# Attention values on one core: the last 17 keys as four 32-row tiles, straight from the transposed blocks

## The reference

```python
def reference(x, ctx_1024, mask, g_xattn, g_ffn, Wq, Wk, Wv, Wo, Wg, W1, W2, W3):
    q = (_layernorm(x) @ Wq).reshape(b, -1, 16, 64)
    k, v = (ctx @ Wk).reshape(b, -1, 16, 64), (ctx @ Wv).reshape(b, -1, 16, 64)
    scores = einsum('bthd,bThd->bhtT', q, k) / sqrt(64)
    scores = where(mask, scores, finfo(float32).min)
    x = x + tanh(g_xattn) * (einsum('bhtT,bThd->bthd', softmax(scores), v).reshape(b, t, 1024) @ Wo)
    n = _layernorm(x)
    top_v, top_i = top_k(n @ Wg.T, 2)
    ...
    y = (silu(n @ W1[e].T) * (n @ W2[e].T)) @ W3[e].T        # for each expert e
    x = x + tanh(g_ffn) * sum_e y * w_e
```

## Time and profile before

| | us |
|---|---|
| median of 3 runs | 617.12 |
| lowest, highest | 616.49, 617.38 |
| the profiled execution | 619.6 |
| its span, first to last instruction | 617.5 |
| TensorE busy | 594.6 (96%) |
| VectorE busy | 407.2 (66%) |
| ScalarE busy | 271.2 (44%) |
| GpSimd busy | 308.6 (50%) |
| mean granted TensorE clock | 0.99 |

### The profile page before, as it was taken

How to read it: one execution, slowest core, us unless ns; L and a number is a source line. 1 busy time by engine, 2 the same in 40 slices (tenths; PEclk the granted TensorE clock), 3 DMA queues, 4 the chain that set the end, 5 groups by cost and what they waited for, 6 DMA issues and landing times.

```text
span 617.5 us, 10982 instructions
## 1 busy us (share of the span) xinstructions
PE 594.6 (96%) x2914; PEld 348.6 (56%) x2915; DVE 407.2 (66%) x1271; ACT 271.2 (44%) x711; POOL 308.6 (50%) x272
## 2 busy tenths in 40 slices
PE   8999899999999999999999999999999999999993
PEld 5444464656556565555655565656656665666562
DVE  3777988898988989988899976257363322332221
ACT  3755665666565665665656554212421122112210
POOL 3753545565565698564796653612364322222221
PEclk9999999999999999999999989999999999999998
DMA  8936676676767879688787774899676443233312
GB/s 308 340 80 144 137 165 144 144 183 150 165 141 182 172 190 208 130 181 181 152 207 157 167 166 111 251 320 321 159 140 151 64 63 54 42 51 52 50 20 31
DMA packets 114243, 93.74 MB, mean 152 GB/s; under 512 B 38528, under 2 KB 108032, under 8 KB 114176
## 3 DMA queue, kind: packets, MB, share of 16 engines
q1 hardware_dynamic: 92096, 70.37, 47.2%
q10 hardware_dynamic: 15360, 13.64, 10.1%
q0 software_dynamic: 6720, 8.95, 8.8%
HBM read 27.72 MB, written 12.36 MB: 65 GB/s over the span
## 4 chain that ended last, share of the span: by engine, by line
PE 70%; DVE 15%; issue 5%; DMA 3%; ACT 3%; SPq 2%; ACTq 1%; POOL 0%; DVEq 0%; POOLq 0%
PE ps_s L1702 19%; PE ps_o L1518 12%; PE ps_o L1730 9%; PE ps_s L1469 9%; DVE blocksT L1185 5%; PE ps_a L1528 5%; DVE probs L1173 5%; PE ps_t L1406 4%; PE ps_t L1723 2%; ACT probs L748 2%; PE ps_o L1483 2%; PE ps_a L1406 2%; PE ps_t L1469 2%; PE ps_a L1437 1%; DMA out_dram<-yg,ids 1%
## 5 line engine op out<-in xcount | busy, mean ns | idle before, releaser
L615 POOL TENSOR_TENSOR probs<-probs,inv_sum 128x802 f32<-128x802 f32 x128 | 194.9, 1524 | 138.1 <-DVE inv_sum L1162 136.9
L748 ACT ACTIVATE probs<-probs,neg_max 128x401 f32<-128x401 f32 x256 | 159.3, 624 | 111.7 <-DVE neg_max L1173 111.6
L1702 PE MATMUL ps_s<-w_sb,xgT 128*128 x288 | 135.3, 593 | 0.0
L1173 DVE CUSTOM_DVE_ANT_0 probs<-ps_s,biases 128x401 f32<-128x401 f32 x215 | 116.0, 570 | 20.3 <-PE ps_s L1469 19.7
L1185 DVE STREAM_TRANSPOSE blocksT<-probs 128x832 f32<-128x832 f32 x124 | 129.0, 1040 | 0.3 <-POOL probs L615 0.3
L665 POOL DMA_INDIRECT out_dram<-yg,ids x36 | 56.1, 1558 | 141.2 <-DVE yg L1344 101.7
L1518 PE MATMUL ps_o<-probsT,v_sb 128*64 128x512 f32 x496 | 114.3, 603 | 0.0
L1469 PE MATMUL ps_s<-kT,qT 64*128 64x201 f32 (+1 forms) x860 | 109.4, 350 | 3.4 <-DVE neg_max L1173 2.7
L1469 PEld LDWEIGHTS ps_s<-kT,qT 64*128 64x128 f32 x860 | 85.0, 189 | 44.2 <-issue 28.8
L884 ACT COPY gatedT<-ps_t 128x512 f32<-128x512 f32 x36 | 21.1, 585 | 151.6 <-PE ps_t L1723 151.6
L1334 DVE TENSOR_TENSOR gated<-ps_s,silu 128x512 f32<-128x512 f32 x36 | 24.8, 690 | 86.8 <-PE ps_s L1702 82.3
(11 more groups left out here) (182 smaller groups left out, 526.1 us busy)
## 6 DMA issues: line engine op xcount, KB each, us to landing
probsT<-blocksT SPq DMA_DIRECT2D x276, 96.0 KB
probsT<-blocksT SPq DMA_DIRECT2D x92, 128.0 KB
probsT<-blocksT ACTq DMA_DIRECT2D x96, 96.0 KB
xg_blocks<-x_regrouped SPq DMA_DIRECT2D x156, 32.0 KB, 2.2
probsT<-blocksT ACTq DMA_DIRECT2D x32, 128.0 KB
w_sb<-W1T_dram SPq DMA_DIRECT2D x8, 512.0 KB, 5.0
w_sb<-W2T_dram SPq DMA_DIRECT2D x8, 512.0 KB, 5.9
w_sb<-W3T_dram SPq DMA_DIRECT2D x8, 512.0 KB, 8.2
```

What stands on the lines that cost most here:

```text
L615: pool.tensor_tensor(duo, duo, inv_sum[:, u:u + 2].unsqueeze(2).to_broadcast([P, 2, LASTK]), ALU.mult)\
L748: act.activation(probs[:, b, 0:LASTK], probs[:, b, 0:LASTK], ACT.Exp, bias=neg_max[:, b:b + 1], scale=-1.0, accum_out=sum_exp[:, b:b + 1]) ...
L1173: dve.tensor_tensor_reduce(probs[:, b, 0:LASTK], scores_bank(u)[:, 0:LASTK], biases[:, tile, :], HD ** -0.5, 3e38, ALU.add, ALU.min, neg_m ...
L1702: mm = pe.matmul(bank[:, :], xgT[:, buf, k, :], w_sb[:, bass.ds(expert, 1), (n * KT + k) * FH:(n * KT + k + 1) * FH].squeeze(1), start=(k ...
```

## The change

The three full strips are multiplied as before. The tail (the 13th block, 17 keys and 15 of zeros) isn't carried into `probsT` any more: `tail(c, b, ...)` takes block 12 of `blocksT` where it lies, on partitions 32b to 32b + 31, as a 32-row tile against 128 query columns, four times (b = 0 to 3) for each of the two heads. For that the values of the last 17 keys must stand on all four groups of 32 partitions. So a padded context `ctx_tail` with the 17 keys four times over is made by GpSimd at the start, and `values` multiplies it at full width.

Row tiles of different rows must not write one bank at the same time. In chunks 4 to 28 (`PAIRED`) the query columns are split over two banks, `ps_o` and `ps_t[1]`, strips are cut into halves of 256 columns, and tails 0 and 2, then 1 and 3 run side by side in the two banks. Tails into one bank wait for each other (`tail_added`). In chunks 0 to 3, 29 and 30 all goes into one bank, with a strip or half a strip between two tails. The last chunk has its tail in a tile of its own (`last_tail`), 32 rows by 512 columns.

`ps_t[1]` also takes the query projections. So TensorE waits in the middle of the value matmuls until ScalarE has copied the queries (`q_ready`), and before a later query projection until the outputs are copied (`oT_ready`). ScalarE's query copy moves ahead of the exponentials, and its output copy is two copies of half the width in these chunks. `blocksT` has three places (`home`) instead of two, as a chunk's blocks must stay until its value matmuls are done; VectorE's transposes wait for the value matmuls of three chunks before instead of the transfers of two chunks before. The buffers are laid out anew. Gone are the memsets of the fourth strip in `probsT` and of the tail in `v_sb`.

```diff
+PAIRED = range(4, 29)
...
-                probsT = sb("probsT", [P, 2, NS, 4, 2, P], F32, fast)
-                blocksT = sb("blocksT", [P, 2, BLOCKS, 2, P], F32, fast)
+                probsT = sb("probsT", [P, 2, NS - 1, 4, 2, P], F32, fast)
+                last_tail = sb("last_tail", [P, 4, 2, P], F32, fast)
...
+                blocksT = sb("blocksT", [P, 3, BLOCKS, 2, P], F32, fast)
...
-        def pv_bank(c):
-            return ps_s[0] if c == CHUNKS - 1 else ps_o
+        def pv_bank(c, half=0):
+            return ps_s[0] if c == CHUNKS - 1 else ps_t[1] if half and c in PAIRED else ps_o
+
+        def home(c):
+
+            return (c + 1) % 3
...
-            strips = len(range(g, BLOCKS, 4))
-            eng.dma_start(probsT[32 * g:32 * g + 32, c % 2, 0:strips, b, :, :],
-                          blocksT[32 * b:32 * b + 32, c % 2, g::4, :, :]).then_inc(probsT_in[c % 2], 16)
+            eng.dma_start(probsT[32 * g:32 * g + 32, c % 2, :, b, :, :],
+                          blocksT[32 * b:32 * b + 32, home(c), g:BLOCKS - 1:4, :, :]).then_inc(probsT_in[c % 2], 16)
...
-            pool.memset(v_sb[:, NS - 1, :, :], 0.0).then_inc(pads_ready, 1)
+            pool.memset(ctx_tail[:, :, :], 0.0).then_inc(pads_ready, 1)
...
+            for k in range(KT):
+                pool.tensor_copy(ctx_tail[:, k, :].rearrange("p (b j) -> p b j", j=32)[:, :, 0:TAIL],
+                                 ctx_last[:, k, LASTK - TAIL:LASTK].unsqueeze(1).to_broadcast([P, 4, TAIL]))\
+                    .then_inc(ctx_tail_ready, 1)
...
-                    pool.memset(probsT[:, :, NS - 1, :, :, :], 0.0).then_inc(pads_set, 1)
+                    pool.sem_inc(pads_set, 1)
...
+                if c in PAIRED:
+                    for half in range(2):
+                        done = act.copy(oT[:, c % 4, :].rearrange("p (t b n) -> p t b n", t=GT, b=4)[:, :, 2 * half:2 * half + 2, :],
+                                        pv_bank(c, half)[:, 0:GQ // 2].rearrange("p (b t n) -> p t b n", b=2, t=GT))
+                    done.then_inc(oT_ready, 1)
...
+                if n % 4 == 0 and QUERIES_T < n // 4 + 2 <= CHUNKS:
+
+                    queries(n // 4 + 1)
                 if n < DUOS:
                     exps(n)
-                if n % 4 == 0 and QUERIES_T < n // 4 + 2 <= CHUNKS:
-                    queries(n // 4 + 1)
...
-                if t == 0 and c >= 2:
-                    dve.wait_ge(probsT_in[c % 2], 16 * REGROUP * (c // 2))
+                if t == 0 and c == 2:
+
+                    dve.wait_ge(v_ps, 2 * NS)
+                if t == 0 and c >= 3:
+                    dve.wait_ge(pv_ready, c - 2)
...
-                for s in (2 * part, 2 * part + 1):
+            def strip(c, s, bank, b0, b1, last=False):
+
+                c0 = 2 if bank is ps_t[1] else 0
+                for odd in range(2):
+                    mm = pe.matmul(bank[odd * HD:(odd + 1) * HD, (b0 - c0) * P:(b1 - c0) * P], v_sb[:, s, 2 * (c % HP) + odd, :],
+                                   probsT[:, c % 2, s, b0:b1, odd, :], start=(s == 0), stop=last)
+                return mm
+
+            def tail(c, b, bank, last=False):
+
+                q0 = 32 * b
+                col = (b - 2 if bank is ps_t[1] else b) * P
+                for odd in range(2):
+                    mm = pe.matmul(bank[odd * HD:(odd + 1) * HD, col:col + P], v_sb[q0:q0 + 32, NS - 1, 2 * (c % HP) + odd, :],
+                                   blocksT[q0:q0 + 32, home(c), BLOCKS - 1, odd, :], start=False, stop=last)
+                return mm
...
+                n = sum(1 if i in PAIRED else 3 for i in range(c))
+                if c in PAIRED:
+
+                    strip(c, 0, first, 0, 2)
+                    strip(c, 1, first, 0, 2)
+
+                    pe.wait_ge(q_ready, min(c + 5, CHUNKS))
+                    strip(c, 0, second, 2, 4)
+                    tail(c, 0, first)
+                    tail(c, 2, second).then_inc(tail_added, 1)
+                    strip(c, 1, second, 2, 4)
+                    strip(c, 2, first, 0, 2)
+                    pe.wait_ge(tail_added, n + 1)
+                    tail(c, 1, first, last=True)
+                    tail(c, 3, second)
+                    mm = strip(c, 2, second, 2, 4, last=True)
+                elif c < CHUNKS - 1:
+
+                    strip(c, 0, first, 0, 4)
+                    tail(c, 0, first).then_inc(tail_added, 1)
+                    strip(c, 1, first, 0, 4)
+                    pe.wait_ge(tail_added, n + 1)
+                    tail(c, 1, first).then_inc(tail_added, 1)
+                    strip(c, 2, first, 0, 2)
+                    pe.wait_ge(tail_added, n + 2)
+                    tail(c, 2, first).then_inc(tail_added, 1)
+                    strip(c, 2, first, 2, 4)
+                    pe.wait_ge(tail_added, n + 3)
+                    mm = tail(c, 3, first, last=True)
...
+                    if c - 5 in PAIRED:
+
+                        pe.wait_ge(oT_ready, c - 4)
                     queries(c)
```

More of the change, by code:

```diff
@@ L165, in build @@
                     mask8 = sb("mask8", [P, NT, SKP], U8, early)
-                probsT = sb("probsT", [P, 2, NS, 4, 2, P], F32, fast)
-                blocksT = sb("blocksT", [P, 2, BLOCKS, 2, P], F32, fast)
+                probsT = sb("probsT", [P, 2, NS - 1, 4, 2, P], F32, fast)
+                last_tail = sb("last_tail", [P, 4, 2, P], F32, fast)
+                with ExitStack() as filling:
+                    wv_sb = sb("wv_sb", [P, KT, H * HD], F32, filling)
+                    xn = sb("xn", [P, GT, D], F32, filling)
+                    ctx_tail = sb("ctx_tail", [P, KT, P], F32, filling)
+                blocksT = sb("blocksT", [P, 3, BLOCKS, 2, P], F32, fast)
                 ctx_last = sb("ctx_last", [P, KT, LASTP], F32, fast)
@@ L175, in build @@
                 inv_sum = sb("inv_sum", [P, RING_P], F32, fast)
-                wk_sb = sb("wk_sb", [P, KT, H * HD], F32, fast)
-                xn = sb("xn", [P, GT, D], F32, fast)
             with ExitStack() as slow:
@@ L317, in settled @@
             eng.wait_ge(pads_set, 2)
+            eng.wait_ge(ctx_tail_ready, KT)
             eng.wait_ge(k_ready, 4)
@@ L752, in values @@
                 s, half = c // 2, c % 2
-                w = TAIL if s == NS - 1 else P
-                act.wait_ge(pads_ready, 2)
                 act.wait_ge(v_ps, c + 1)
-                act.copy(v_sb[0:w, s, 8 * half:8 * half + 8, :],
-                         ps_o[0:w, :].rearrange("p (h d) -> p h d", h=8)).then_inc(v_ready, 1)
+                act.copy(v_sb[:, s, 8 * half:8 * half + 8, :],
+                         ps_o[:, :].rearrange("p (h d) -> p h d", h=8)).then_inc(v_ready, 1)
             def outputs(c):
@@ L762, in outputs @@
                     act.wait_ge(wo_ps, 2 * ((c - 4) // 2) + 2)
-                act.copy(oT[:, c % 4, :].rearrange("p (t b n) -> p t b n", t=GT, b=4),
-                         pv_bank(c)[:, :].rearrange("p (b t n) -> p t b n", b=4, t=GT)).then_inc(oT_ready, 1)
+                if c in PAIRED:
[3 more added lines that the diff above has]
+                    done.then_inc(oT_ready, 1)
+                else:
+                    act.copy(oT[:, c % 4, :].rearrange("p (t b n) -> p t b n", t=GT, b=4),
+                             pv_bank(c)[:, :].rearrange("p (b t n) -> p t b n", b=4, t=GT)).then_inc(oT_ready, 1)
             def move_turned(d):
@@ L769, in move_turned @@
                 bank, c, t = turned_banks(d)[1], CHUNKS - 1, d % GT
-                act.copy(probsT[:, c % 2, 0:NS - 1, :, 1, 32 * t:32 * t + 32],
+                act.copy(probsT[:, c % 2, :, :, 1, 32 * t:32 * t + 32],
                          bank[:, 0:LAST_STRIP].rearrange("p (s b j) -> p s b j", s=NS - 1, b=4)).then_inc(turned[1], 1)
-                act.copy(probsT[0:32, c % 2, NS - 1, :, 1, 32 * t:32 * t + 32],
+                act.copy(last_tail[0:32, :, 1, 32 * t:32 * t + 32],
                          bank[0:32, LAST_STRIP:].rearrange("p (b j) -> p b j", b=4)).then_inc(turned[1], 1)
@@ L1475, in values @@
                 s, half = c // 2, c % 2
-                w = TAIL if s == NS - 1 else P
+                keys = ctx_tail if s == NS - 1 else ctx_last
+                k0 = 0 if s == NS - 1 else s * P
+                if s == NS - 1 and half == 0:
+                    pe.wait_ge(ctx_tail_ready, KT)
                 if c == 0:
@@ L1482, in values @@
                 for k in range(KT):
-                    mm = pe.matmul(ps_o[0:w, :], ctx_last[:, k, s * P:s * P + w],
+                    mm = pe.matmul(ps_o[:, :], keys[:, k, k0:k0 + P],
                                    wv_sb[:, k, half * 512:(half + 1) * 512], start=(k == 0), stop=(k == KT - 1))
@@ L1491, in turn @@
                 pe.wait_ge(q_ready, CHUNKS)
+                if d == LAST_DUO:
+                    pe.wait_ge(oT_ready, PAIRED[-1] + 1)
                 if d == DUOS - 1:
@@ new lines, in tail, with probs_v @@
+            def tail(c, b, bank, last=False):
```

(26 more changed lines are left out.)

35 lines of the change are left out of this document (11 added, 24 removed).

## The result

| | before, us | after, us |
|---|---|---|
| median of 3 runs | 617.12 | 635.88 |
| lowest, highest | 616.49, 617.38 | 634.87, 635.96 |
| span of the profiled execution | 617.5 | 633.9 |

The ratio is 1.0296, interval 1.0279 to 1.0313: slower by 18.8 us, where 8.8 was forecast. The sign was right, the size missed by 10 us, and 635.9 lies above the top of the range, 634.5.

What follows compares the result with a forecast made beforehand. TensorE's work was taken to set the pace in most attention chunks. Paired chunks 3.8, early single ones 3.3, query copy 0.45, values -0.4 and end 1.6 made +8.8 us: median 617.12 to 626.0 us, range 615.5 to 634.5.

Steps and rivals of the forecast that it cites:

- The shape changes: Value matmuls: each tile-shape change costs 0.155 us, 0.10 gap and 0.05 load; paired chunks +0.21 us, single ones +1.10.
- the rival with row tiles in turn: Paired chunks' tails: the four tiles don't run together, 0.44 us more a chunk, 633.8 us; chance 0.11.
- the free change of shape: Borders of strips and tails: 128 to 32 rows costs nothing while columns stay 64, 609.8 us, faster; chance 0.16.
- The values of the last keys: Their projection becomes 128 columns wide; a gap or first load of 0.1 us goes in four places: -0.4 us.
- Chunk 1's extra 1.06 us: Chunk 1's added value-matmul time, forecast 1.10 us, goes into TensorE's 1.19 us of waiting behind it.
- The early chunks: Single chunks 0, 2 and 3 on the chain add 1.10 us each, 3.3 us.
- The paired ones: 18 paired chunks on the chain add 0.21 us each, 3.8 us.
- The end: Chunks 29 to 31 add 2.36 us to TensorE, less 0.74 us idle before the experts: +1.6 us.
- The query copy: Mid-chunk, TensorE waits 0.15 us for ScalarE's copy in nine chunks, three on the chain: 0.45 us; none in others.
- The clock: Rival: the low-clock stretch, about 3.4 us, goes (622.6 us) or comes twice (629.4 us); chance 0.14.
- Output copy in two halves: ScalarE's split copy adds perhaps 0.1 us before the exponentials; zero on the chain, 0.7 us in all if cover is gone.

Runs made afterwards that it cites:

- e9_copy_first_bank_later: Changed kernel with query copy ahead of ScalarE's two transfer issues and the first bank's third strip ahead of the wait: 625.62 us, 1.012 of before.
- e8_two_banks_copy_first: Kernel before with value sums halved over two banks, no 32-row tiles, query copy ahead of ScalarE's two transfer issues: 618.97 us, 1.001 of before.
- after_again: The changed kernel unaltered, run and traced once more beside the experiments: 636.16 us, 1.0285 of before.
- e5_one_bank: Changed kernel with no paired chunks, every chunk using one bank with four tails one after another: 648.29 us, 1.051 of before.

## Why the prediction was wrong

**The shape changes: right, step by step.** All starts of the changed kernel's own matmuls agree with the terms.

- A paired chunk without a wait takes 3.80 us, forecast 3.80; a single one 4.64, forecast 4.69; the last one, from 409.47 to the next group at 413.20, 3.73, forecast 3.74.
- A pair of tails takes 142.17 - 141.79 = 0.38 us with its border: the forecast had 2 x 0.109 + 0.155 = 0.37. The four tiles run together, the rows of the two banks within 0.02 us of each other (141.79 and 141.81 in chunk 7), so the rival with row tiles in turn is out. So is the free change of shape: 0.10 us stands at every inner border. The rule of the Trainium skill, TensorEngine Tiling (Array Packing), section Key Properties, that a change of tiling mode drains TensorE, agrees with that number.
- The values of the last keys: chunk 0's value matmuls start 0.41 us earlier than before, against -0.4.
- Chunk 1's extra 1.06 us went into the wait behind it, as forecast: the output projection there starts without one (74.97), where it had waited 1.19 us.

The trace of `e9_copy_first_bank_later`, which has no wait for the copy, gives the sums: TensorE starts chunk 4 2.75 us after before (forecast 3.3 - 0.4 = 2.9) and chunk 27 5.99 after. The early chunks are right to 0.15 us. The paired ones give 3.24 us, 15 chunks x 0.215. Of the forecast's 18 chunks, 3.8 us, two (27 and 28) lie behind this point, so that it had 16 here and 6.3 us in all; the sixteenth is chunk 24, from which to the next it is 11.24 us before and 11.26 in this trace, so its 0.21 was absorbed as in 23 and 25. Chunks 27 and 28 run through the stretch of lower clock, which differs between traces, and no number here shows their 0.4 us apart from it.

**The end: right in kind, 0.6 us too much.** The wait of 0.74 us for the transfer is gone, the twelve passes being followed at once:

```profile
418.49 5.31 PE L1783 MATMUL ps_s<-w_sb,xgT 128*128 x12
423.64 0.60 PE L1804 MATMUL ps_t<-ident,gated 128*128 128x128 f32 x4
```

The answer to the earlier trace rows has 5.15 us between these two where 5.89 stood. Chunks 30 and 31 add 13.66 - 12.30 = 1.36 us, forecast 1.10 + 0.16 = 1.26. But chunk 29's 1.06 us is mostly absorbed: chunk 30 starts 10.46 us behind chunk 29 in the changed kernel and started 10.10 behind it before, because TensorE waited there for chunk 29's output copy before and doesn't now:

```profile
384.93 0.39 PE L1448 MATMUL ps_o<-counts,ones 128*128 128x40 f32 x2 [0.47 <-ACT oT L763]
```

So the end costs 0.36 + 1.36 - 0.74 = +1.0 us where +1.6 was forecast: a wait behind a group that grows was not looked for, though chunk 1's was.

**The query copy: the step that failed.** The prediction took ScalarE's queue from the exponentials' end at 202.78 us straight to the copy, and came to a wait of 0.15 us in nine chunks, three of them on the chain, 0.45 us in all. Measured: 20 of the 24 chunks from 5 to 28 wait, 12.2 us and 11.2 us in two traces. Three things were missed; the first stood in the rows of before.

- Two transfer issues of 0.59 and 0.63 us stand between the exponentials and the copy in ScalarE's program. They aren't counted as ScalarE's busy time, and the prediction listed only ACT rows. With them the copy of chunk 13 would have been costed at 203.29 to 203.85, a wait of 0.6 instead of 0.15 (measured 0.85, with one routing instruction between).
- A late copy isn't absorbed. "The exponentials end about when the matmuls begin" gave zero for the ordinary chunks; it is 0.33 us there in each, since the next exponentials depend on scores behind the wait, so the whole cycle moves and the copy is late by the same amount again. Seven such chunks make 2.3 us.
- The issue isn't always 0.6 us. One of the 92 in this stretch of the changed kernel takes 1.67 us, and its copy costs 1.73. That couldn't be read before: the 96 issues of ScalarE in the same stretch of before all take under 0.9 us.

The span's 16.4 us add up so: 6.0 for the shapes as far as chunk 27; 11.5 of waits before it, of which 1.2 are absorbed, since TensorE starts chunk 27 16.2 us later than before; 0.8 less for chunks 27 and 28, with the lower clock and the last two waits in it; 1.0 for the end. Timed on one chip, the change is 636.16 us and `e9_copy_first_bank_later` 625.62, so the copy cost 10.5 us; without it the changed kernel stands 7.4 us over before. The forecast less its 0.45 us said 8.35.

**The clock.** The rival let the half-clock stretch go or come twice. It stayed, at another place. Around the granted clock was 0.5 for 6.8 us; in the changed kernel it is for 3.4, from 384.9 to 388.3, behind the same wait of 1.37 us:

```profile
382.02 1.95 PE L1465 MATMUL ps_a<-wg_sb,rowsT 128*128 128x8 f32 x16 [1.37 <-DVE xs L1238]
...
385.97 1.97 PE L1539 MATMUL ps_o<-probsT,v_sb 128*64 128x256 f32 x8
387.73 0.88 PE L1539 MATMUL ps_t<-probsT,v_sb 128*64 128x256 f32 x4
```

The eight passes take 387.73 - 385.97 = 1.76 us instead of 0.92. The shorter stretch speaks for the changed kernel, so it explains nothing of the miss. Nor is its length the change's: `before_again`, the kernel before unaltered, has 3.4 us of it too, and starts chunk 30 1.57 us earlier than the first trace of before.

**Output copy in two halves, transfers, GpSimd, VectorE's new waits: zero, as forecast.** In `e8_two_banks_copy_first` the two halves are in, and the time is that of before.

## What to carry to other kernels

When a wait is moved onto an engine's instruction, read everything that stands ahead of that instruction on its engine in program order, the sequencer's transfer issues included: they fill no busy time and held the copy here by half a microsecond a chunk, 10 us in all. A wait inside a loop whose next round depends on the waiter isn't paid once but every round; ask what absorbs it, and if nothing does, multiply it by all the rounds. And one change should be costed in its two halves: the tiles cost 7 us, the second bank nothing, and the place of one copy more than both.

## What the runs showed of the hardware

- **Four tiles of 32 x 64 run together.** Two row tiles times two column tiles, writing two banks, start within 0.02 us of each other, and a pair of tails costs 0.38 us with its border. Without them the chunk is 1.06 us shorter: for 17 keys the streaming is 0.44 of it, and the rest is four borders.
- **A transfer issue on ScalarE takes 0.62 us at the median and now and then 1.1 to 2.3.** From 107 to 372 us the two traces of before have 96 issues each and none over 0.9 us; `after_again` has none either, and the other ten traces have one to four, `e5_one_bank` with its single bank among them. What makes them long isn't settled. Where the copy stands ahead of them they cost nothing: `e8_two_banks_copy_first` has three of 1.8 to 2.0 us and the time of before.
- **The hold at the end of attention**, with ScalarE, VectorE and SyncE late together by 2 to 4 us, in seven traces of thirteen, all seven from two of three chips. Open.
